# Attention block on one core: GpSimd sums each step's probabilities head by head

## The reference, cut to what matters

```python
xn = (xg - mean) * rsqrt(var + EPS)            # group norm, 32 groups; then * gn_w + gn_b
qkv = einsum('oc,bct->bot', qkv_w, xn) + qkv_b
q, k, v = split(qkv.reshape(b * 8, 3 * 64, T), 3, axis=1)
weight = softmax(einsum('bct,bcs->bts', q * scale, k * scale), axis=-1)
a = einsum('bts,bcs->bct', weight, v).reshape(b, c, T)
hout = einsum('oc,bct->bot', proj_w, a) + proj_b
return (xn + hout).reshape(b, c, h, w)
```

## Time and profile before

| what | value |
|---|---|
| median of 3 runs | 3774.83 us |
| profiled execution, its own time | 3774.18 us |
| its span | 3772.5 us |
| TensorE busy | 3699.3 us (98%) |
| GpSimd busy | 3001.7 us (80%) in 1639 instructions |
| ScalarE busy | 2867.9 us (76%) |
| VectorE busy | 2246.3 us (60%) |
| mean granted TensorE clock | 0.997 of full speed |

### The profile page before, as it was taken

The page is one execution under the profiler, slowest core; times in us unless marked ns, Lnnn a source line. Parts: engine busy times, 40 slices in busy tenths (PEclk is TensorE's granted clock), DMA queues, the critical chain, the costliest instruction groups (busy, mean ns, idle before and its releaser), DMA issues.

```text
span 3772.5 us, 74528 instructions
## 1 busy us (share of the span) xinstructions
PE 3699.3 (98%) x30004; PEld 2263.6 (60%) x30004; DVE 2246.3 (60%) x2820; ACT 2867.9 (76%) x4037; POOL 3001.7 (80%) x1639
## 2 busy tenths in 40 slices
PE   6999999999999999999999999999999999999998
PEld 4565565655856556565675656556567565656556
DVE  4566557656555565765646565666655656565653
ACT  2777777787577777778757777777876777777885
POOL 0788888888388888888838888888874888888994
PEclk9999999999999999999999999999999999999999
DMA  2000012011400001201140000110223000000014
GB/s 80 14 23 22 21 36 69 23 56 38 146 21 19 24 23 32 73 19 58 44 139 19 23 23 17 52 53 27 68 63 104 23 21 21 22 19 19 20 37 138
DMA packets 133673, 165.02 MB, mean 44 GB/s; under 512 B 61648, under 2 KB 110800, under 8 KB 132816
## 3 DMA queue, kind: packets, MB, share of 16 engines
q1 hardware_dynamic: 133328, 160.26, 13.5%
HBM read 122.17 MB, written 38.04 MB: 42 GB/s over the span
## 4 chain that ended last, share of the span: by engine, by line
PE 91%; ACT 3%; DMA 2%; DVE 2%; issue 1%; SPq 1%; POOL 0%; POOLq 0%; ACTq 0%; DVEq 0%
PE oacc L611 29%; PE scores L590 23%; PE pool_bank L538 13%; PE aux_banks L560 12%; PE pool_bank L550 7%; PE scores L690 4%; PE pool_bank L577 1%; ACT probs L795 1%; ACT scores L808 1%; DVE maxima L911 1%; DMA out<-probs 1%; PE scores L538 1%; DMA neg_rows<-neg_cols 1%; POOL denom L1157 0%; DVE o_norm L1018 0%
## 5 line engine op out<-in xcount | busy, mean ns | idle before, releaser
L1157 POOL TENSOR_TENSOR denom<-denom,probs 128x768 f32<-128x768 f32 x1536 | 2825.5, 1840 | 425.0 <-ACT probs L795 235.0
L911 DVE TENSOR_REDUCE maxima<-aux_banks 128x2 f32<-128x512 f32 x1728 | 1656.0, 958 | 1314.9 <-PE aux_banks L560 1281.9
L795 ACT ACTIVATE probs<-scores 128x768 f32<-128x768 f32 x1728 | 1311.2, 812 | 676.1 <-PE scores L590 668.1
L808 ACT ACTIVATE scores<-seeds 128x768 f32<-128x768 f32 x1728 | 1342.6, 823 | 19.3 <-PE scores L598 10.0
L611 PE MATMUL oacc<-probs,vals 128*64 128x384 f32 x6912 | 1283.0, 492 | 0.0
L611 PEld LDWEIGHTS oacc<-probs,vals 128*64 128x64 f32 x6912 | 455.0, 136 | 523.3 <-issue 381.9
L560 PE MATMUL aux_banks<-k_hi,q_hi 64*128 64x512 f32 (+1 forms) x3456 | 684.0, 391 | 20.7 <-DVE maxima L911 18.8
L560 PEld LDWEIGHTS aux_banks<-k_hi,q_hi 64*128 64x128 f32 x3456 | 322.8, 183 | 548.9 <-issue 443.8
L590 PE MATMUL scores<-q_hi,k_hi 64*128 64x384 f32 x3456 | 599.6, 343 | 17.3 <-ACT scores L808 17.0
L590 PE MATMUL scores<-q_lo,k_hi 64*128 64x384 f32 x3456 | 587.6, 335 | 0.0
L590 PE MATMUL scores<-q_hi,k_lo 64*128 64x384 f32 x3456 | 587.5, 335 | 0.0
(11 more groups left out here) (91 smaller groups left out, 1476.4 us busy)
## 6 DMA issues: line engine op xcount, KB each, us to landing
seeds<-neg_rows SPq DMA_DIRECT2D x96, 384.0 KB, 3.5
xtile<-x SPq DMA_DIRECT2D x72, 384.0 KB, 3.2
att<-o_norm SPq DMA_DIRECT2D x96, 192.0 KB, 1.9
probs<-x SPq DMA_DIRECT2D x24, 768.0 KB, 4.5
out<-probs SPq DMA_DIRECT2D x24, 768.0 KB, 3.7
xtile<-att SPq DMA_DIRECT2D x12, 768.0 KB, 4.6
att_raw<-att SPq DMA_DIRECT2D x12, 768.0 KB, 6.3
neg_rows<-neg_cols SPq DMA_DIRECT2D x384, 0.8 KB
```

Source lines behind the costliest of these rows:

```text
L795: a(prob(s).rearrange("p (h n) -> p h n", n=N), scores[:, s % 2, :, 0:N], ACT.Exp, scale=SCALE).then_inc(probs_ready, 1)
L808: a(scores[:, s % 2, :, 0:N], seeds[blk % 2][:, :].rearrange("p (e n) -> p e n", n=N), ACT.Copy).then_inc(seeded, 1)
L911: v.tensor_reduce(maxima[:, :, qt, kc], aux_banks[:, :, 0:UNIT_KEYS[kc % 2]], AX.X, ALU.max)\
L1157: gp.tensor_tensor(acc, acc, prob(s), ALU.add).then_inc(added, 1)
```

## The change

Each add of a step becomes two adds, one over the 384 columns of each head. Only the second of the two counts up `added`, so all who wait for `added` wait for both. The first of the two takes the waits that the single add had, and the second has no wait.

```diff
                 if kt == 1:
                     if blk >= 2:
                         pool.wait_ge(o_normed, PRIMED + BLOCKS * b + blk - 1)
-                    gp.tensor_tensor(acc, prob(s - 1), prob(s), ALU.add).then_inc(added, 1)
+                    gp.tensor_tensor(acc[:, 0:N], prob(s - 1)[:, 0:N], prob(s)[:, 0:N], ALU.add)
+                    gp.tensor_tensor(acc[:, N:2 * N], prob(s - 1)[:, N:2 * N], prob(s)[:, N:2 * N], ALU.add)\
+                      .then_inc(added, 1)
                 else:
                     pool.wait_ge(added, PRIMED + ADDS * (BLOCKS * b + blk) + kt - 1)
-                    gp.tensor_tensor(acc, acc, prob(s), ALU.add).then_inc(added, 1)
+                    gp.tensor_tensor(acc[:, 0:N], acc[:, 0:N], prob(s)[:, 0:N], ALU.add)
+                    gp.tensor_tensor(acc[:, N:2 * N], acc[:, N:2 * N], prob(s)[:, N:2 * N], ALU.add)\
+                      .then_inc(added, 1)
```

## The result

The changed kernel takes 3781.85 us (median of 17 runs, 3780.39 to 3784.33), and the kernel before 3775.43 us (17 runs, 3773.8 to 3779.32). The ratio is 1.0017, with a 95% interval of 1.001 to 1.0023: slower by 6.4 us, or 0.17%. I had forecast 40 us. That is clear of the noise and just under the 0.2% that I had named as the least that can be told. The profiled execution took 3780.39 us with a span of 3778.7, against 3774.18 and 3772.5 before.

What follows compares the result with a forecast made beforehand. GpSimd's adds were taken to have little slack and to bound the last six blocks; 30.1 us in the last batch plus 10.2 in the other three, on 3774.18, gave 3815 us, range 3779 to 3930.

Steps and rivals of the forecast that it cites:

- d: On GpSimd, the extra time of two adds of 384 columns over one of 768; forecast at 0.177 us.
- The bounds, 0.037 and 0.240: Limits of d in us: below from memsets' start distances, above from the mask's fixed part paid in full.
- the fixed part of the mask: GpSimd's 128-column mask, 0.345 us less 0.105 for columns: 0.240 us; less 0.063 overlap it gave d.
- the full price: Rival: each second add pays its whole fixed part, d over 0.21, GpSimd bounds throughout; 3917 us at 0.240; chance 0.22.
- the slack: GpSimd's waits beyond turnarounds: 59.6 us in each of the first three batches, 42.1 in the last.
- The sum itself: Per batch of 408 adds: 72.2 us more GpSimd work, less slack, and less carried lag outside the last batch; 40.3 us total.
- the last batch's term: In the last batch, 72.2 us less 42.1 of slack leaves 30.1 us, delaying the end one for one.
- lag carried: GpSimd may run 9.2 us late into the projection between batches, whose 55 us without adds wipe it out.
- the rival that makes it a gain: Listed third: shorter adds let VectorE's multiply through sooner, making the kernel faster, perhaps by 10 us; chance 0.03.
- The forecast case: d from 0.093 to 0.21 us on GpSimd's adds, giving 3782 to 3868 us; chance 0.60.
- The hold-up of GpSimd by the multiply: VectorE's multiply may delay a second half once a block, 0 to 0.4 us; costed at 0.
- my limits of 2.08 and 2.2: GpSimd's pitch per pair, forecast 2.16 us: under 2.08 only the tail moves, over 2.2 every batch is longer.

Runs made afterwards that it cites:

- e2: Against the kernel before: two adds a step in the last six blocks of the last batch only, one elsewhere; 3790.6 us, ratio 1.0042.
- e6: Against the kernel before: two adds a step everywhere but in the last six blocks of the last batch; 3767.5 us, ratio 0.9978.
- e12: The same kernel as e6, timed again against the kernel before; 3766.13 us, ratio 0.9974.
- e5: Against the kernel before: three adds of 256 columns a step, everywhere; 4004.82 us, ratio 1.0607.
- e3: Kernel before, single adds, with VectorE's multiply replaced by a one-operand transpose of the same tile (output left without denominators); 3766.33 us, ratio 0.9978.
- e4: Changed kernel with a count for each half, the first half waiting only for the step before's first half; 3938.32 us, ratio 1.0426 to the kernel before.
- e7: Changed kernel (two adds a step) with VectorE's multiply replaced by the one-operand transpose; 3779.24 us, ratio 1.001 to the kernel before.
- e9: e4 (a count for each half) with VectorE's multiply replaced by the one-operand transpose; 3785.01 us, ratio 1.003 to the kernel before.

## Why the prediction was right or wrong

**The direction, and the place of most of the loss, were right.** GpSimd is 80% busy, has 0% of the chain, and yet bounds the last six blocks; the loss is made there, and e2 shows it. The first three batches were to lose 3.4 us each, and gained 7.7 together. The measured 0.17% lies within 0.2%, which I had given 0.15. The time lies inside my wide range, 3 us above its lower end of 3779. That the sign came out right is in part luck, as it is the difference of a loss of 14 us and a gain of 7.7 that I had at nothing.

**The size of d was off.** I had 0.177 us and it is 0.137. The bounds, 0.037 and 0.240, held. The first step that failed is the fixed part of the mask, 0.240 us, taken for that of an add. I had got it with the 0.105 us that a memset takes for the columns, which is 0.83 ns a column. The records of 768 and 384 columns give (1.831 - 1.006) / 384 = 2.148 ns a column and 0.181 us fixed, and the overlap is 0.042 us, not 0.063: 0.181 - 0.042 = 0.139. The mask was no guide to that. The page of the Trainium skill that I weighed, GPSIMD Engine Reference, section 3.1, gave 0.231 fixed, an estimate by its figure for 2048 columns; the trace doesn't agree with that as a fixed part. (The rival that a d of 0.231 belongs to is the second one, the full price, and not the third as I had written.) Since the slack is 0.146 us an add in the first three batches, 0.04 us decided whether they lose anything.

**The sum itself came out close, in part by luck.** With 0.137 a batch needs 408 x 0.137 = 55.9 us more. In the last batch that leaves 55.9 - 42.1 = 13.8, and 14.0 were measured. But these 14.0 are net of what VectorE's multiply gave back in this batch. The six blocks take 203.0 and 202.8 us in e6 and e12, and 218.4 in the changed kernel, so the halves cost 15.5 us there. In the others 55.9 is below the 59.6 of slack, so they lose nothing, instead of 3.4 us each. (Two figures of the prediction are a little off, without effect: 35.85 / 17 - 1.985 is 0.124 and not 0.126, and the slack of the last batch is 42.0.) Of the 34 us by which the forecast was too high, 30.1 - 13.8 = 16.3 are in the last batch's term and 10.2 in that of the others, both from d. e5 shows the sum's own error at twice this d, at least 4 to 11 us a batch: less slack can be used, and less lag carried (7.2 us, not 9.2).

**The remaining 8 us are the second step that failed, the one that I called off the path.** I had costed the multiply's shorter wait as a gain "of some 0.5 us, off the path", and held the rival that makes it a gain, with 10 us, at 0.03. It is 0.74 us each, and in most blocks it is indeed off the path, as the lead of the exponentials stands still there. But at two or three places in a batch VectorE has no slack, and e3 shows that taking all of this wait away is worth 8.3 us. I had argued from VectorE's 2% of the chain. A wait of TensorE for VectorE of 0.79 us, as above, is on the chain with what VectorE did before it, and 2% of the chain are 75 us, room for all of it. The forecast case and this rival were not exclusive: both came true, in different batches, and I should have added them.

**The hold-up of GpSimd by the multiply** was put at 0 to 0.4 us a block. In e4's and the changed kernel's traces an add that follows a multiply is longer by 0.13 us behind a turnaround (1.13 to 1.14 where others have 1.00) and by 0.3 inside a run. In the kernel before it is as long (1.95 where others have 1.83), so it played no part in the difference.

**What would show it.** Waits of TensorE's weight loads at L577 for the adds did appear, 1.6 us in the first three batches and 11.7 in the last; a pitch of 2.113 us lies between my limits of 2.08 and 2.2, yet the time, 3781.85 us, lies where I had put a pitch under 2.08, 3778 to 3782.

## What to carry to other kernels

Ask of an engine how much idle time it has beyond its turnarounds, for each stretch, and not how busy it is: here 20% idle meant 0.13 us an instruction, and none at the end. Where an instruction of one engine holds up the other's, as here, a long instruction of the one is a wait of the other. Cut it up where there is slack and the other engine has none, leave it whole where it is the bound, and don't close the gaps between its instructions without asking who gets in through them. Effects that act in different stretches are summed, even where they were set up as rivals.

## What the runs showed of the hardware

VectorE's multiply, with two SBUF operands, waits for GpSimd's running add. In the kernel before, the changed one and e4 it ends 0.41 to 0.42 us after an add's record in 252 of the 256 cases in which it met an add, and in the other four at most 0.53. A transpose of the same tile, with one operand, takes 0.567 to 0.580 us in all of its 96 cases in e3, e7 and e9, whatever GpSimd does. The Trainium skill says so for this pair (SBUF — State Buffer, section "Who interferes with whom"): a VectorE instruction with two SBUF inputs contends with a GpSimd instruction that reads SBUF. The trace agrees, with 1.67 us against 0.57.

The number of operands is not the whole rule. The TENSOR_SCALAR at L982 has one SBUF operand, of four columns. It took 0.17 us while GpSimd was idle, and 1.60 in each of the three other batches, where it ended 0.02 to 0.03 us after an add:

```profile
L982 DVE TENSOR_SCALAR small<-small x4: 170/1599/1604, 22.6 to 2557.9; 128x4 f32<-128x4 f32 x4
```

With the halves its median is 0.50. Since the edit of e3 changes the operation together with the number of operands, no run separates the two.

What I had not expected is that VectorE can be passed over. When the adds follow without a turnaround, a multiply waited through the running one and five more (e4, 5.67 us), and once for 18.6 us. What was passed over once stayed out until GpSimd ran dry: all 32 multiplies in e4, and in e9 an instruction that waited 41.57 us. In e4 others got in after the first half that they met, at 0.87 us. What decides between the two isn't settled: of the multiplies that began 0.54 us after the start of a half, some were passed over and some were not. No experiment moved that moment.
